# Low parts of W3 for experts 4 to 7 made on GpSimd instead of VectorE

## The reference

```
logits = xn @ Wg;  top_w, top_i = top_k(logits, 2);  top_w = softmax(top_w)
h = xn @ W1[e];  g = xn @ W2[e];  y = (silu(h) * g) @ W3[e]
out = sum over the token's two experts e of  weight(e) * y(e)
```

## Time and profile before

| what | us |
|---|---|
| median of 3 runs | 635.36 |
| the profiled execution, its own time | 635.06 |
| its span | 633.3 |
| TensorE busy | 609.5 (96%) |
| VectorE busy | 448.1 (71%) |
| GpSimd busy | 361.1 (57%) |
| ScalarE busy | 341.3 (54%) |
| eight W3 low subtractions on VectorE | 9.8 in all, from 305.2 to 335.9 |

### The profile page before, as it was taken

How to read it: one execution, slowest core, us unless ns; L and a number is a source line. 1 busy time by engine, 2 the same in 40 slices (tenths; PEclk the granted TensorE clock), 3 DMA queues, 4 the chain that set the end, 5 groups by cost and what they waited for, 6 DMA issues and landing times.

```text
span 633.3 us, 16654 instructions
## 1 busy us (share of the span) xinstructions
PE 609.5 (96%) x5181; PEld 479.3 (76%) x5181; DVE 448.1 (71%) x1134; ACT 341.3 (54%) x483; POOL 361.1 (57%) x453
## 2 busy tenths in 40 slices
PE   8899999999999999999999899999999999999995
PEld 8665666666676666666788788888888888888884
DVE  6877878797878776697895557666676666666673
ACT  3668878787878777764663333333333333333331
POOL 4256464747474655557176366666656566666645
PEclk9999999999999999999999999999999999999998
DMA  4653555646444444562943556566565555656553
GB/s 133 173 128 104 132 162 116 182 95 161 109 118 112 106 126 99 157 180 87 374 82 74 107 116 124 118 125 120 126 124 119 120 119 124 122 121 122 121 97 43
DMA packets 73346, 80.36 MB, mean 127 GB/s; under 512 B 12368, under 2 KB 61392, under 8 KB 73264
## 3 DMA queue, kind: packets, MB, share of 16 engines
q1 hardware_dynamic: 56144, 50.72, 30.5%
q0 software_dynamic: 16704, 28.12, 22.8%
q10 hardware_dynamic: 416, 0.46, 0.3%
HBM read 27.72 MB, written 22.95 MB: 80 GB/s over the span
## 4 chain that ended last, share of the span: by engine, by line
PE 72%; issue 10%; POOL 6%; DVE 5%; DMA 2%; ACT 2%; POOLq 1%; SPq 1%; DVEq 0%; ACTq 0%
PE banks L1325 22%; PE banks L1198 11%; PE banks L1346 10%; PE banks L1179 8%; PE banks L1218 7%; PE banks L1227 4%; PE banks L1262 3%; POOL xg L566 2%; PE banks L1314 2%; PE banks L1247 2%; POOL out L592 1%; PE banks L1288 1%; POOL mark L578 1%; PE banks L1253 1%; ACT T L629 1%
## 5 line engine op out<-in xcount | busy, mean ns | idle before, releaser
L592 POOL DMA_INDIRECT out<-yo,xw x71 | 112.6, 1586 | 102.8 <-DVE yo L1123 82.3
L541 POOL TENSOR_SCALAR_AFFINE_SELECT T<-T 128x512 f32<-128x512 f32 x128 | 81.6, 649 | 98.6 <-ACT T L629 47.2
L1325 PE MATMUL banks<-w12h,xgh 128*128 x284 | 113.3, 399 | 4.2 <-DVE xgl L1101 3.0
L1325 PE MATMUL banks<-w12l,xgh 128*128 x284 | 111.3, 392 | 0.0
L1325 PE MATMUL banks<-w12h,xgl 128*128 x284 | 111.0, 391 | 0.0
L1135 DVE TENSOR_TENSOR hs<-banks,hs 128x512 f32<-128x512 f32 x71 | 49.1, 692 | 87.1 <-PE banks L1325 77.3
L729 ACT ACTIVATE sTh<-banks 128x512 fp32r<-128x512 f32 x71 | 42.4, 599 | 92.4 <-DVE banks L1111 75.3
L566 POOL DMA_INDIRECT xg<-xs_scr,glist x71 | 72.3, 1019 | 25.1 <-issue 21.2
L629 ACT ACTIVATE T<-banks 128x1024 f32<-128x1024 f32 x64 | 62.1, 1023 | 28.2 <-PE banks L1179 24.7
L1198 PE MATMUL banks<-T,vau 128*17 128x512 f32 (+3 forms) x1024 | 75.4, 434 | 0.7 <-POOL T L541 0.7
L536 POOL DMA_INDIRECT xs_scr<-xb,slots x64 | 64.3, 1004 | 20.4 <-issue 12.3
(11 more groups left out here) (186 smaller groups left out, 1223.2 us busy)
## 6 DMA issues: line engine op xcount, KB each, us to landing
hq<-hs SPq DMA_DIRECT2D x244, 64.0 KB
w12r<-w SPq DMA_DIRECT2D x16, 512.0 KB, 4.9
Q<-Q SPq DMA_DIRECT2D x126, 64.0 KB, 2.4
out<-xa SPq DMA_DIRECT2D x16, 256.0 KB
w3r<-w SPq DMA_DIRECT2D x8, 512.0 KB, 8.2
K<-Kt SPq DMA_DIRECT2D x126, 32.0 KB
xa<-x SPq DMA_DIRECT2D x7, 512.0 KB, 4.8
xg<-xs_scr,glist POOLq DMA_INDIRECT x71
```

What stands on the lines that cost most here:

```text
L541: e.affine_select(out=v, in_=v, pattern=[[0, 4], [1, P]], compare_op=ALU.is_ge, fill=-1.0, base=0, channel_multiplier=-1).then_inc(s["g_mk ...
L592: e.indirect_dma_start(out, bass.IndirectOffsetOnAxis(xw[:, t % XR, NE:NE + 1].bitcast(U32), 0), yo[t % 3], None, compute_op=ALU.add).then ...
L1325: i = e.matmul(banks[:, 2 * (t % 2) + m, :], a[:, k, :], w[:, bass.ds(expert[t] * 4 + (2 * k + m), 1), :], start=(k == 0 and n == 0), stop ...
```

## The change

The subtractions for experts 0 to 3 stay on VectorE. Those for experts 4 to 7 are issued by GpSimd, one behind each of `scatter(2)` to `scatter(5)`. They signal a new semaphore, `g_tl`. TensorE's wait ahead of `down(t-1)` is split: `v_tl` up to 4, and from t = 5 to 8 also `g_tl` to t-4.

```
@@ gpsimd_program
+            def w3_low(n):
+                e.wait_ge(s["a_th"], n + 1)
+                e.tensor_tensor(W3l[:, rows(n), :], W3r[:, rows(n), :], W3h[:, rows(n), :].bitcast(F32),
+                                ALU.subtract).then_inc(s["g_tl"], 1)
...
                 scatter(t)
+                if 4 <= t + 2 < NE:
+                    w3_low(t + 2)
@@ vector_program
-                if t + 1 < NE:
+                if t + 1 < 4:
                     w3_low(t + 1)
@@ tensor_program
                     if t <= NE:
-                        e.wait_ge(s["v_tl"], t)
+                        e.wait_ge(s["v_tl"], min(t, 4))
+                        if t > 4:
+                            e.wait_ge(s["g_tl"], t - 4)
                     down(t - 1)
```

More of the change, by code:

```diff
@@ L305, in build @@
                 "a_si", "v_mu", "p_st", "a_st", "v_st", "p_yo", "v_yo", "d_sc0", "d_sc1",
-                "c_hold", "v_hold", "g_hold", "d_hq0", "d_hq1", "v_th")
+                "c_hold", "v_hold", "g_hold", "d_hq0", "d_hq1", "v_th", "g_tl")
         MISC, USED = misc_uses()
```

## The result

The changed kernel took 639.00 us in the median (637.99 to 642.83, 9 runs), the kernel before 635.36 us (634.14 to 637.74, 9 runs). The ratio is 1.0055, with an interval of 1.0031 to 1.0079: slower by about 0.55%. The forecast was 638.7 us.

A forecast was written before the change was run, and what follows sets the result against it. The prediction took TensorE to bound the kernel. GpSimd's delays made `down(7)` 3.3 us late; with 0.1 for a restart, 635.06 + 3.4 = 638.5, and 0.3 more for the median gave 638.7 us, range 635.3 to 641.5.

The forecast's parts named there:

- TensorE is the bound, VectorE costs it one hole of 0.2 us: Between 316 and 345 us TensorE is full but for a wait for `xgl`; filling it gains 0.2 us.
- D: Time of one moved subtraction on GpSimd, taken as 2.0 us from its select's rate for two inputs.
- The upper end of 4.0: Highest estimate for one GpSimd subtraction, from a 664 ns row of 128 elements; as a rival, 646 us, chance 0.08.
- GpSimd's cycle is 3.37 + D: Per iteration, GpSimd's fixed work plus one subtraction: 5.37 us against TensorE's 4.87, losing 0.5 us each for experts 6 and 7.
- GpSimd's first subtraction waits for W12's low part: At expert 4, GpSimd waits for VectorE until 327.97 and ends at 330.0, making `down(4)` 1.0 us late.
- The rival: At `scatter(2)`, GpSimd goes first and holds VectorE: about +2.0 us, 637.4; chance 0.15 together with no lock at all.
- `scatter(3)` is held by the last W12 part: At expert 5, VectorE's subtraction holds the scatter until 332.85, so it ends at 334.3 and `down(5)` is 1.5 us late.
- TensorE idles ahead of `down(4)` to `down(7)`, released by GpSimd: Expected sign on TensorE: idle about 1.0, 1.5, 0.5 and 0.5 us there, until GpSimd's `w3l` is done.
- The sum of +3.3: Start of `down(7)` at 347.25 instead of 343.95, from GpSimd's delays over experts 4 to 7.
- VectorE waits for neither gathers nor scatters: Behind GpSimd's subtractions, later gathers and scatters delay nothing: 3 us is covered, and scatters may be two periods late.
- What is lost stays lost: Behind the stall TensorE is the bound again, 252.95 busy of 261.00 us from 372 us, so nothing is made up.

The follow-up runs named there:

- e6: The changed kernel with GpSimd's subtractions two iterations later and TensorE waiting for them only in iteration 12; ratio 0.9995 to the kernel before.
- e7: As e6, with the small copy `xw` made by ScalarE instead of VectorE; ratio 0.9985 to the kernel before.
- e8: The changed kernel with each GpSimd subtraction ahead of its scatter instead of behind it; ratio 1.0023 to the kernel before.
- e1: The changed kernel, but TensorE waits for all four GpSimd subtractions only in iteration 12, ahead of `down(9)`; ratio 1.0073 to the kernel before.
- e10: The changed kernel with its own waits, each GpSimd subtraction split into four of 128 x 256; ratio 1.0070 to the kernel before.
- e5: The changed kernel itself, run again on another chip; ratio 1.0052 to the kernel before.
- e3: The changed kernel with both edits: TensorE's wait only in iteration 12, and `xw` copied by ScalarE; ratio 1.0048 to the kernel before.
- e9: As e1, with each GpSimd subtraction split into four of 128 x 256; ratio 1.0016 to the kernel before.

## Why the prediction was right, point by point

The number and the pace (GpSimd's cycle against TensorE's) were right. What released TensorE, and the order of the first two subtractions, were not.

- *TensorE is the bound, VectorE costs it one hole of 0.2 us.* Right: e6 and e7 take the four subtractions off VectorE there, and the stretch is 0.3 us shorter.
- *D = 2.0 us, from the select's rate for two streams.* It was 2.41 to 2.43 us (e8, and the changed kernel). By the Trainium skill's figure (GPSIMD Engine Reference, Elementwise — side-by-side cycle accounting), half of 4497 ns, the estimate was 2.25, nearer but also short. The upper end of 4.0 is refuted; whether its row was stretched by a hold is open.
- *GpSimd's cycle is 3.37 + D.* Measured 5.55 where GpSimd isn't held, so 3.12 beside the 2.43: the gap ahead of a gather behind a subtraction is 0.16 and not 0.30, and the 0.10 was not there. The two errors cancel to 0.2 us (5.37 predicted).
- *GpSimd's first subtraction waits for W12's low part.* Wrong way round. In the changed kernel the scatter ended at 327.74, ahead of VectorE's 327.94, and VectorE was held; `down(4)` was late by 0.15 us and not by 1.0. The rival's condition was met: `scatter(2)` began 0.4 us earlier behind `down(3)` than before (0.80 against 1.21). The rival had this order, but priced it at +2.0, because it had VectorE held once. It was held in each of the four iterations.
- *`scatter(3)` is held by the last W12 part.* It was the gathers behind the first two subtractions that were held (1.79 and 1.86 us against 0.99), since W12's parts had been pushed back to there. 0.8 and 0.9 us, where the prediction had one hold that cost 1.0 (334.3 against 331.7 + 1.59).
- *TensorE idles ahead of `down(4)` to `down(7)`, released by GpSimd.* Wrong as to what the trace shows: the waits stood at `sTl` and `xgl`, released by VectorE. Right as to size: growth of the four periods over before is 0.15 + 1.28 + 1.55 + 0.62 = 3.60 us where 3.3 was predicted. The number was near because both mechanisms run at GpSimd's pace. While VectorE is held once per GpSimd cycle, TensorE has GpSimd's period through VectorE (e1); while it waits for `g_tl`, it has it directly (e10). The holds alone cost 3.7 us (e1), both together 3.6 and 4.9 (the change and e5); the wait alone, with the longer work of e10, 4.3.
- *The sum of +3.3.* That it came so near is luck in its terms. GpSimd's chain was 1.7 us longer by the subtractions (four times 0.43) and 0.7 by the gathers' holds; it was 1.0 shorter without the first wait, 0.8 by the gaps (three times 0.25), and 0.4 by the earlier scatter. They nearly cancel. In e5, where the scatter came later, the same stretch lost 4.9 us.
- *VectorE waits for neither gathers nor scatters.* What the sum left out was the subtraction in front of them: `xw` was held until its end three times, for 3.5 us or more. By itself that cost 0.8 us (e6 against e7), since VectorE had time.
- *What is lost stays lost.* Right: 3.6 us up to `down(7)`, and 0.5 more up to `down(8)`, since the last held `xw` made `xgl` late. Behind that a period is 4.4 us in both kernels. That the medians differ by 3.64 us, just what is lost up to `down(7)`, is partly chance: the two profiled runs differ by over 1 us ahead of `down(3)`, and by as much the other way behind `down(8)`.

## What to carry to other kernels

Look at what a moved instruction meets in the iterations where it stands, not at its new engine's share of the span: 3.1 us of fixed work and 2.4 us of new work against a period of 4.87 was enough to lose 3.6 us. A later deadline alone won nothing (e1); a later deadline and a later place together cost nothing (e7). A subtraction on GpSimd also held VectorE's subtractions with both inputs in SBUF and its copy; put it where these aren't on the way to the bound. When two mechanisms give the same number, take each away alone and then both: here neither edit alone won anything, and both together little if anything (e3), because a second hold took the copy's place. Only the rows showed that.

## What was not expected of the hardware

- A VectorE instruction can be held although it is recorded ahead of GpSimd's: by 0.47 to 0.72 us for `xw` in the changed kernel, by 0.53 for W12's low part in e5, by 0.19 us in e8. In each case GpSimd was then in the DMA instruction just ahead of its subtraction. In the kernel before, VectorE's large subtractions run at 1.22 us beside GpSimd's gathers and scatters, so it is the queued subtraction that matters. Where exactly the hold begins stays open.
- VectorE's instructions with an input in PSUM weren't held. `sTl` took its 0.69 us in e3 in the middle of a subtraction of GpSimd's, which ran from the scatter's end at 345.06 to 347.50:

```profile
346.40 0.69 DVE L1123 TENSOR_TENSOR sTl<-banks,sTh 128x512 fp32r<-128x512 f32 x1 [1.86 <-ACT sTh L741]
```

- A subtraction behind a scatter is recorded 1.05 us into it and as 2.95 us long; behind a `mark` it is 2.41 us (e8). Its cost on the queue is 2.4 us in both.
- Quarters did not reliably let VectorE in: they did in e10 and did not in e9. Why is open.
